# The second expert layer of a convolution, attention and expert kernel: products turned, sums over tokens taken along the free side, the product of the means in four column groups, the last products in four row groups

## The reference

```python
# t: a token after normalization, top 2 of 16 experts with softmax gates
h_e[t]   = silu(x[t] @ w1[e].T)            # 128 -> 512
mean_e   = sum of h_e[t] over the tokens routed to e, / max(count_e, 1)
ymean_e  = mean_e @ w2[e].T                # 512 -> 128, one vector per expert
out[t]   = residual[t] + sum_e gate_e[t] * ymean_e
```

## Time and profile before

| | |
|---|---|
| time, median of 3 executions | 3617.76 us (3611.89 to 3627.61) |
| the profiled execution's own time | 3635.59 us |
| its span, first to last instruction | 3633.8 us |
| PE, DVE, ACT, POOL busy in it | 2827.6, 2208.3, 1549.9, 1040.7 us |
| mean granted TensorE clock | 0.884 of full speed |

### The profile page before, as it was taken

One profiled execution on the slowest core, in us unless ns is written; L12 is line 12 of the kernel. 1 busy time (PEld: TensorE's weight loads), 2 busy tenths in 40 slices (PEclk: granted clock), 3 DMA queues, 4 the chain that ended last, 5 costly groups with the idle time before them and its releaser, 6 DMA issues. The chain is left out here.

```text
span 3633.8 us, 65093 instructions
## 1 busy us (share of the span) xinstructions
PE 2827.6 (78%) x20886; PEld 1553.7 (43%) x20887; DVE 2208.3 (61%) x4232; ACT 1549.9 (43%) x3274; POOL 1040.7 (29%) x1360
## 2 busy tenths in 40 slices
PE   6777849999999999996599119558888888619998
PEld 3334503433343334332598117435555555403336
DVE  5774547777777777772222116547777777526771
ACT  1113516666666666664355003424444444404440
POOL 0002300122222222223233752214565565620000
PEclk8998959999999999999799559868998888859995
DMA  2002442132213232310322113332333223021123
GB/s 76 0 0 102 184 84 39 37 52 45 51 39 53 42 54 39 53 25 11 103 61 60 41 41 111 103 55 54 60 64 63 61 58 62 24 90 50 51 57 117
DMA packets 209243, 215.62 MB, mean 59 GB/s; under 512 B 33456, under 2 KB 185201, under 8 KB 209009
## 3 DMA queue, kind: packets, MB, share of 16 engines
q1 hardware_dynamic: 187008, 178.05, 21.8%
q0 software_dynamic: 14336, 25.72, 2.7%
q10 hardware_dynamic: 7680, 8.93, 0.7%
HBM read 129.26 MB, written 81.90 MB: 58 GB/s over the span
## 5 line engine op out<-in xcount | busy, mean ns | idle before, releaser
L1539 ACT ACTIVATE attn_exps<-attn_sbank 128x392 f32<-128x392 f32 x1600 | 704.6, 503 | 499.3 <-PE attn_sbank L1456 493.6
L1581 DVE TENSOR_REDUCE attn_mx<-attn_rot 128x1 f32<-128x784 f32 x768 | 722.3, 967 | 191.8 <-PE attn_rot L1469 188.0
L1469 PE MATMUL attn_rot<-attn_k,attn_q 96*128 96x392 bf16 x1536 | 401.6, 344 | 97.1 <-DVE attn_mx L1581 64.6
L2223 ACT ACTIVATE dil_exps<-dil_sbank 128x512 f32<-128x512 f32 x512 | 289.2, 597 | 407.3 <-PE dil_sbank L2121 338.1
L1456 PE MATMUL attn_sbank<-attn_q,attn_k 99*128 99x392 bf16 x1536 | 450.1, 333 | 12.3 <-ACT attn_exps L1539 11.1
L1496 PE MATMUL attn_acc<-attn_exps,attn_v 128*32 128x392 f32 x3584 | 348.4, 500 | 0.0
L2274 DVE TENSOR_REDUCE dil_mx<-dil_rot 128x4 f32<-128x1024 f32 x256 | 307.6, 1219 | 55.4 <-PE dil_rot L2131 53.2
L2131 PE MATMUL dil_rot<-dil_k,dil_q 96*128 96x256 bf16 x1024 | 174.2, 299 | 120.3 <-DVE dil_mx L2274 83.2
L1456 PEld LDWEIGHTS attn_sbank<-attn_q,attn_k 99*128 99x128 bf16 x1536 | 148.8, 98 | 270.1 <-ACT attn_exps L1539 133.9
L2661 PE MATMUL silu_ph<-silu_route_w,silu_xT 128*128 x424 | 237.7, 645 | 22.6 <-issue 11.2
L1469 PEld LDWEIGHTS attn_rot<-attn_k,attn_q 96*128 96x128 bf16 x1536 | 117.5, 99 | 303.5 <-DVE attn_mx L1581 201.6
(11 more groups left out here) (370 smaller groups left out, 4863.5 us busy)
## 6 DMA issues: line engine op xcount, KB each, us to landing
attn_q<-q_pieces SPq DMA_DIRECT2D x192, 98.0 KB
attn_k<-k_pieces SPq DMA_DIRECT2D x192, 98.0 KB
silu_x<-silu_rows SPq DMA_DIRECT2D x212, 64.0 KB
dil_q<-dil_q_pieces SPq DMA_DIRECT2D x192, 66.0 KB
dil_k<-dil_k_pieces SPq DMA_DIRECT2D x192, 66.0 KB
q_pieces<-qkv_piece SPq DMA_DIRECT2D x16, 588.0 KB, 3.1
k_pieces<-qkv_piece SPq DMA_DIRECT2D x16, 588.0 KB, 3.2
v_rows<-qkv_v SPq DMA_DIRECT2D x16, 476.0 KB, 3.8
```

Source lines behind the costliest of these rows:

```text
L1469: ins = nc.tensor.matmul(rot[b][:, hf, 0:HS], q[nxt.side][g][0:QROWS, j, c * P:(c + 1) * P], k_[nxt.side][g][0:QROWS, j, cols], start=True ...
L1539: nc.scalar.activation(e_[:, n % NP, :], sbank[(n + t.side) % 3][:, 0:HS], ACT.Exp, scale=A_DIM ** -0.5).then_inc(s_ex, 1)
L1581: nc.vector.tensor_reduce(into, rot[b][:, :, 0:HS], AX.XY, ALU.max).then_inc(s_free, 1)
L2223: nc.scalar.activation(e_[:, k % NP, :], sbank[k % 3][:], ACT.Exp, scale=D_DIM ** -0.5).then_inc(s_ex, 1)
```

## The change

In `experts_silu` the product is turned: the piece of `w1` is now the weights, and the turned tile the data, so the 512 middle values lie on partitions (four groups of 128) and the tokens along the free side. This takes a weight operand at a fixed place, so GpSimd copies the expert's `w1` (128 x 512) to one of four buffers `ws`, three tiles ahead, as in the GELU stage. ACT takes SiLU in two pieces of 256. DVE sums over the tokens with one `tensor_reduce` to 128 x 4 (`part`), and GpSimd adds that to the expert's four columns of `sums`. `acc`, its memset and the 64 products with ones are gone. `w2` has memory of its own and is loaded in `route_tail` behind `w1`. The means are laid out 32 wide, the product with `w2` runs as four accumulations, one in each group of 32 output partitions, and a product with the constant `same` adds the four quarters and repeats the result in each group of 32 partitions. In `finish` the gates lie in four groups of 32 partitions, so that the products of four images stand in four row groups of TensorE; the loops are written out. What is added up is the same; counts of the experts, gates and tables are as before.

```diff
@@ route_tail @@
-                for dst, src in early:
-                    act.dma_start(dst, src).then_inc(s_early, 16)
+                for dst, src, sem in early:
+                    act.dma_start(dst, src).then_inc(sem, 16)
@@ experts_silu @@
-        w2 = w1[:, :, :].rearrange("p e (c d) -> p e c d", c=4)
-        acc = m.sb("acc", [TILE, E, FF])
...
+        mean = m.sb("mean", [P, E, 4, 32])
+        part = [m.sb(f"part{n}", [P, 4]) for n in two]
+        y4 = m.sb("y4", [P, P])
+        ws = [m.sb(f"ws{n}", [P, FF]) for n in range(NX)]
...
+                sp.dma_start(same[:], a["same"]).then_inc(s_w, 16)
...
-                sp.dma_start(gates_t[:], gates_d).then_inc(s_gates, 16)
-                sp.wait_ge(s_ph, NT)
-                for e in range(E):
-                    sp.dma_start(w2[:, e], a["L3_w2"][e].rearrange("(c f) d -> f c d", c=4)).then_inc(s_w2, 16)
-                sp.wait_ge(s_gates, 16)
+                for g in range(4):
+                    sp.dma_start(gates_t[32 * g:32 * g + E, :, :], gates_d.rearrange("e (i g) s -> e g i s", g=4)[:, g]).then_inc(s_gates, 16)
+                sp.wait_ge(s_gates, 16 * 4)
+
+            @block.gpsimd
+            def _(pool):
+
+                def copy(n, at):
+                    e = pool.value_load(table[0:1, 1, at], min_val=0, max_val=E - 1)
+                    nc.gpsimd.tensor_copy(ws[n][:], w1[:, bass.ds(e, 1), :].rearrange("p o n -> p (o n)")).then_inc(s_ws, 1)
+
+                def tile(t):
+                    if t.lo + AHEAD < NT:
+                        if t.lo >= 1:
+                            pool.wait_ge(s_ph, 4 * t.t)
+                        copy((t.lo + AHEAD) % NX, bass.ds(t.t + AHEAD, 1))
+                    if 2 <= t.lo <= NT + 1:
+                        e = pool.value_load(table[0:1, 1, bass.ds(t.t - 2, 1)], min_val=0, max_val=E - 1)
+                        pool.wait_ge(s_part, t.t - 1)
+                        pool.wait_ge(s_sum, t.t - 1)
+                        into = sums[:, bass.ds(e, 1), :].rearrange("p o c -> p (o c)")
+                        nc.gpsimd.tensor_tensor(into, part[t.lo % 2][:], into, ALU.add).then_inc(s_sum, 1)
+
+                nc.gpsimd.memset(sums[:], 0.0).then_inc(s_sum, 1)
+                pool.wait_ge(s_early, 16 * E)
+                for t in range(AHEAD):
+                    copy(t, slice(t, t + 1))
+                run_tiles(pool, NT, tile)
@@ experts_silu, PE @@
-                        e = pe.value_load(table[0:1, 1, bass.ds(t, 1)], min_val=0, max_val=E - 1)
-                        if lo >= 2:
-                            pe.wait_ge(s_h, t - 1)
+                        pe.wait_ge(s_ws, t + 1)
                         pe.wait_ge(s_xT, t + 1)
-                        nc.tensor.matmul(ph[n][:, :], xT[n][:], w1[:, bass.ds(e, 1), :].rearrange("p o f -> p (o f)"), start=True, stop=True).then_inc(s_ph, 1)
+                        for c in range(4):
+                            if lo >= 2 and c % 2 == 0:
+                                pe.wait_ge(s_h, 2 * t - 3 + c // 2)
+                            nc.tensor.matmul(ph[n][c // 2][:, c % 2 * TILE:(c % 2 + 1) * TILE], ws[lo % NX][:, c * P:(c + 1) * P], xT[n][:], start=True, stop=True).then_inc(s_ph, 1)
...
-                        ins = nc.tensor.matmul(psum_[:, 4 * e + c:4 * e + c + 1], acc[:, e, c * P:(c + 1) * P], onesc[:], start=True, stop=True)
...
-                        ins = nc.tensor.matmul(pm[0:E, 0:P], mean[:, e, c, :], w2[:, e, c, :], start=(e == 0 and c == 0), stop=(e == E - 1 and c == 3))
+                        ins = nc.tensor.matmul(pm[32 * c:32 * c + 32, 0:P], mean[:, e, c, :], w2[:, e, c, :], start=(e == 0), stop=(e == E - 1))
                 ins.then_inc(s_y, 1)
+                pe.wait_ge(s_y4, 1)
+                nc.tensor.matmul(pr[:, 0:P], same[:], y4[:], start=True, stop=True).then_inc(s_rep, 1)
@@ experts_silu, DVE @@
-                nc.vector.memset(acc[:], 0.0)
...
-                        e = dve.value_load(table[0:1, 1, bass.ds(t - 1, 1)], min_val=0, max_val=E - 1)
-                        dve.wait_ge(s_h, t)
...
-                        nc.vector.tensor_tensor(part, h[1 - n][:], part, ALU.add).then_inc(s_acc, 1)
+                        dve.wait_ge(s_h, 2 * t)
+                        if lo >= 3:
+                            dve.wait_ge(s_sum, t - 1)
+                        nc.vector.tensor_reduce(part[1 - n][:], hT[1 - n][:], AX.X, ALU.add).then_inc(s_part, 1)
@@ finish, PE @@
-                with pe.Fori(0, B // 4) as i:
-                    for j in range(4):
-                        pe.wait_ge(s_add, 4 * i + j + 1)
-                        for h in range(2):
-                            ins = nc.tensor.matmul(pa[j][:, h, 0:HS], ymean[:], gates_t[:, 4 * i + j, h * HS:(h + 1) * HS], start=True, stop=True)
-                        ins.then_inc(s_p, 1)
+                for i in range(B // 4):
+                    for h in range(2):
+                        for j in range(4):
+                            if i > 0 and h == 0:
+                                pe.wait_ge(s_add, 4 * i + j - 3)
+                            ins = nc.tensor.matmul(pa[j][:, h, 0:HS], ymean[32 * j:32 * j + SILU.n, :], gates_t[32 * j:32 * j + SILU.n, i, h * HS:(h + 1) * HS], start=True, stop=True)
+                            if h == 1:
+                                ins.then_inc(s_p, 1)
```

More of the change, by code:

```diff
@@ L1096, in pool_done, with route_tail @@
             pool.wait_ge(self.s_sct[j], self.SCT * PAIRS)
-def route_tail(nc, a, ex, xs, table, keep, stage, early, s_early, positions=None, counts=None):
+def route_tail(nc, a, ex, xs, table, keep, stage, early, positions=None, counts=None):
     E, K, NT = ex.n, ex.picks, ex.tiles
@@ L2681, in tile @@
                     if lo < NT:
-                        act.wait_ge(s_ph, t + 1)
-                        if lo >= 2:
-                            act.wait_ge(s_acc, t - 1)
-                        nc.scalar.activation(h[n][:], ph[n][:, :], ACT.Silu).then_inc(s_h, 1)
+                        for k in two:
+                            act.wait_ge(s_ph, 4 * t + 2 * k + 2)
+                            if k == 0 and lo >= 2:
+                                act.wait_ge(s_part, t - 1)
+                            nc.scalar.activation(hT[n][:, 2 * k:2 * k + 2, :].rearrange("p c n -> p (c n)"), ph[n][k][:, 0:2 * TILE], ACT.Silu).then_inc(s_h, 1)
                 run_tiles(act, NT, tile)
@@ L2791, in softmax_and_routed @@
         s_early = m.sem("expert_weights")
-        early = [(w1b[:, e, :], a["L2_w1b"][e]) for e in range(GELU.n)]
-        early += [(w2[:, e, :, :], a["L2_w2"][e].rearrange("(c f) d -> f c d", c=4)) for e in range(GELU.n)]
-        route_tail(nc, a, GELU, xs, table, keep, "r1", early, s_early, positions=positions)
-        experts_gelu(nc, a, xs, ys, table, w1b, w2, s_early)
+        s_w2 = m.sem("second_weights")
+        early = [(w1b[:, e, :], a["L2_w1b"][e], s_early) for e in range(GELU.n)]
+        early += [(w2[:, e, :, :], a["L2_w2"][e].rearrange("(c f) d -> f c d", c=4), s_w2) for e in range(GELU.n)]
+        route_tail(nc, a, GELU, xs, table, keep, "r1", early, positions=positions)
+        experts_gelu(nc, a, xs, ys, table, w1b, w2, s_early, s_w2)
         combine(nc, a, R, ys, positions, gates)
@@ L2812, in dilated_and_routed @@
         s_early = m.sem("expert_weights")
-        early = [(w1[:, e, :], a["L3_w1"][e]) for e in range(SILU.n)]
-        route_tail(nc, a, SILU, xs, table, keep, "r2", early, s_early, counts=counts)
-        experts_silu(nc, a, xs, table, counts, ymean, w1, s_early, gates_d, gates_t, s_gates)
+        w2 = m.sb("w2", [P, SILU.n, 4, P])
+        s_w2 = m.sem("second_weights")
+        early = [(w1[:, e, :], a["L3_w1"][e], s_early) for e in range(SILU.n)]
+        early += [(w2[:, e, :, :], a["L3_w2"][e].rearrange("(c f) d -> f c d", c=4), s_w2) for e in range(SILU.n)]
+        route_tail(nc, a, SILU, xs, table, keep, "r2", early, counts=counts)
+        experts_silu(nc, a, xs, table, counts, ymean, w1, w2, s_early, s_w2, gates_d, gates_t, s_gates)
         finish(nc, R, gates_t, ymean, out)
@@ L2908, in layouts @@
         d[f"tiles{ex.n}"] = np.pad(np.arange(ex.tiles, dtype=np.float32).reshape(-1, rows).T, ((0, P - rows), (0, 0)))
-    d["only"] = np.eye(SILU.n, dtype=np.float32).reshape(1, -1)
+    d["only"] = np.eye(SILU.n, 32, dtype=np.float32).reshape(1, -1)
+    d["same"] = (k[:, None] % 32 == k[None, :] % 32).astype(np.float32)
     return {n: np.ascontiguousarray(x) for n, x in d.items()}
```

91 lines of the change are left out of this document (41 added, 50 removed).

## The result

The changed kernel takes 3649.3 us (3642.4 to 3652.4, 5 runs), the kernel before 3617.8 beside it: 1.0083 of before, 95% interval 1.0059 to 1.0107, so slower by 21 to 39 us. The forecast was 3645, within 3605 to 3680. The profiled execution took 3649.3 as well, with a span of 3647.5 us; the profiled one of before was 17.8 over its median. So the two spans differ by 13.7 us only: the unchanged stages ahead of the last routing ended 14.9 us earlier in this profile.

The account below looks back on a forecast made before the run. The prediction took SP's instruction stream, 1.28 us a tile, to bound the kernel before, and GpSimd's, 1.68, the changed one. +79.4 - 34.0 - 17.8 = +27.6 us moved the median from 3617.8 to 3645 us, range 3605 to 3680.

Parts of the forecast that it names:

- The tile cost of 1.68 us: Tile loop: GpSimd's two table reads at 0.68 us each plus small operations and loop turn, against 1.28 before; bounds 1.36 to 1.9.
- the rival theory: Tile loop, posed with the experiments: waits between sum, reduction and SiLU over two `part` buffers set the pace; no chance given.
- Rival (c): Tile loop: GpSimd's sequencer isn't the bound and SP's 1.28 us a tile stays; -54.2 us, 3564 us; chance 0.12.
- The signs: Tile loop trace: GpSimd never waiting, `silu_ph` waiting for its copy, SP waiting, reduction near 0.69 us; 1.6 to 1.75 a tile.
- Start of the tiles: After the last routing: DVE's memset goes, barrier 0.5 us later, first pieces at about 3266.8; through the tiles' end +79.4 us.
- Sums and means' product: After the last tile: products with ones gone, means' product 6.5 us in column groups; 11.9 for 45.9, -34.0 us.
- Finish: Final products and adds to the residual: four row groups side by side, 22.8 for 40.6, -17.8 us; bounds 0 and -21.
- the forecast's three terms: Finish: DVE starts at 2.8 us, four adds take 3.8 four times, DVE idles 1.6 three times; 22.8 us.
- Rival (b): Finish: row groups don't overlap, so PE's 40 us stay; +17.8, 3663 us; chance 0.08.
- rival (d): Tile loop: PE's clock stays low, 2.1 us a tile; +87, 3732 us; chance 0.04.
- rival (e): Tile loop: GpSimd's table reads last 0.3 us longer when two stand close; +124, 3769 us; chance 0.01.
- The sum: Whole kernel: +79.4 for the tiles, -34.0 for sums and means' product, -17.8 for the finish, together +27.6 us.

Follow-up runs that it names:

- the four buffers: The changed kernel with four `part` buffers for two, so DVE's reduction waits for the sum of four tiles back: 3643.3 us, 1.0076 of before.
- the kernel that began at half clock: The kernel before with only the change's end (means' product in four quarters, finish in row groups with loops written out): 3591.7 us, 0.9913 of before.
- the last kernel: The changed kernel without the range test on GpSimd's and SP's table reads, and with the finish's products ordered image by image: 3548.4 us, 0.9805 of before.
- the run with one read: The changed kernel without GpSimd's second table read, every tile's part added to expert 0's columns: 3562.0 us, 0.9837 of before.
- the run with three reads: The changed kernel with a third GpSimd table read per tile, its value unused: 3765.6 us, 1.0414 of before.

## Why the prediction was right, point by point

- **The tile cost of 1.68 us, set by GpSimd's sequencer**: right, and shown three ways (a read less, a read more, the test taken out of each read), with the rival theory ruled out by the four buffers. Rival (c) falls. The parts were off and made up for each other: a read costs about 0.63, not 0.68, which leaves 0.42 for the rest instead of 0.32. That the sum met 1.68 so closely is luck.
- **The signs**: two of them were put wrongly. That the sequencer would be seen "never waiting" was said too simply, since the trace lists GpSimd's idle time before the copy as a wait for PE. And `silu_ph` waits more for `silu_xT` (28.1 us) than for the copy (20.8), which the prediction named as a sign that it is wrong. By the list of waits alone it would have been rejected; the pace and the experiments uphold it. The reduction took 0.686 us, and SP now waits (62.9 of 251 us, for `silu_px`), both as forecast.
- **Start of the tiles**: first pieces 5.5 us behind the barrier's end (3254.29 - 3248.82) as forecast, for 9.2 before. The barrier itself was mis-sized: +2.9 us and not +0.5. ACT was done with its 32 loads at 3243.95, as forecast early enough, and SP with its zero rows at 3243.49, 5.3 us ahead of the barrier's end; before, SP was done at 3258.74, 2.0 us ahead of it. What SP waits for then is the landing of the zero rows. Its waits in the changed kernel (3226 to 3250) and in the one before (3240 to 3262), us in total, times, longest:

```profile
SPq L1139 <- DMA silu_rows<-r_zrow: 4.5, 1, 4.5
```

```profile
SPq L1139 <- DMA silu_rows<-r_zrow: 1.2, 1, 1.2
```

  In the kernel before with the new end, whose `w2` isn't loaded there, it is 1.2 us as well, and in the eleven other runs that load it there 4.2 to 4.9. So the zero rows land later behind the loads of `w2`, a term that the prediction didn't have. The transfers still ran at 228 GB/s from 3244.0 to 3248.8, against 39 in the last 1.7 us of before; whether queues or memory are what they share was not tested.
- **Sums and means' product, 11.9 for 45.9**: 11.5. The product took 5.8 us of a forecast 6.5, and the run with one column group shows that the groups do it.
- **Finish, 22.8 for 40.6**: 21.4 = 1.58 + 4 x 3.62 + 3 x 1.78, the forecast's three terms at 2.8, 3.8 and 1.6. DVE started earlier because the first 16 products ran at full clock, 1.60 us with 1.00 granted; the forecast had counted on half clock, and the kernel that began at half clock took 2.93. Rival (b) falls. At half clock the products in one row group took 0.65 us each (16 of them from 3629.39 to 3639.84, granted 0.50), in four groups 2.93/16 = 0.18 (granted 0.52), which is 3.6 times. The Trainium skill (TensorE: Matmul & The Clock Gate, Part 3) has 3.07 for four row tiles of 32 rows and 512 columns, so this case's figure, with 392 columns of fp32, is higher.
- **Clock**: rival (d) falls. The granted clock was 1.00 in the steady tiles with PE busy 75%.
- **Table reads 0.3 us longer**, rival (e): 0.288 and 0.287 us at the two lines, so it falls.
- **The sum**: +28.5 us in the profiles for +27.6, with the barrier 2.4 us over its term and the finish 1.4 under. That the misses cancel is luck too.

What stays open: what holds the last kernel at 1.22 us a tile. GpSimd's reckoning gives just that, but PE was busy 167.9 of 175 us there, and no run took them apart. Nor did a run change SP's stream alone in a kernel at 1.28 us a tile. That SP sets that pace in the kernel before rests on the prediction's count of its steps, and on the same 1.28 in the run with one read, where PE's work for a tile is another.

## What to carry to other kernels

Count each sequencer's steps per tile before moving a lookup to an engine that looks idle. An engine that is busy 48% of the time can set the pace once two register reads and their range tests stand in its stream, and the list of waits then names its neighbours. Before moving such work, take out steps that aren't needed: leaving out the range test (the table holds only values in range, by its construction) was worth more here than any place for the read that was tried. Where a big rewrite moves the time little, time its parts on the old kernel: the new end alone was worth 30 us.

## What the hardware did that was not expected

- A register load of two elements takes 0.51 us on GpSimd and 0.47 on SP, for 0.29 and 0.27 with one: it is paid nearly by the element.
- The idle time of an engine whose sequencer is the bound appears before whichever instruction the stream reaches late, and is listed as a wait for an engine that had long been done: 0.96 us before, for the copy at 3401.49 shown above.
- With PE busy 133 of 200 us the granted clock fell to a mean of 0.88 in the run with three reads, and was 1.00 with 149.6 of 200 in the run with four buffers.
